# Score products of eight heads summed by identity matmuls one tile ahead, first norm two tiles ahead, w1 parts over ten tiles

## The reference

```python
kv = (ctx @ W_kv.T + b_kv).reshape(B, S, 16, 16, 2); k, v = kv[..., 0], kv[..., 1]
qh = layernorm(x).reshape(B, S, 16, 16)
attn = softmax(einsum('bshd,bstd->bsht', qh, k) / 4, axis=-1)
x = x + tanh(g_xattn) * (einsum('bsht,bstd->bshd', attn, v).reshape(B, S, 256) @ W_out.T + b_out)
y = layernorm(x)
probs = softmax(y @ gate_w.T, axis=-1)            # (16, 256, 8)
g, m = top_k(probs.transpose(0, 2, 1), 64)         # each expert takes 64 tokens of a batch row
h = gelu(y[m] @ w1[e], exact) @ w2[e]              # 256 -> 1024 -> 256
x = x + tanh(g_ffn) * scatter_add(g * h)
```

## Time and profile before

| | us |
|---|---|
| median of 3 runs | 724.87 (723.82 to 727.46) |
| the profiled execution's own time | 725.79 |
| its span, first to last instruction | 723.8 |
| PE busy | 637.5 (88%) |
| VectorE busy | 614.1 (85%) |
| ScalarE busy | 433.7 (60%) |
| POOL busy | 549.6 (76%) |
| mean granted TensorE clock | 0.936 |

### The profile page before, as it was taken

One profiled execution on the slowest core, in us unless ns is written; L12 is line 12 of the kernel. 1 busy time (PEld: TensorE's weight loads), 2 busy tenths in 40 slices (PEclk: granted clock), 3 DMA queues, 4 the chain that ended last, 5 costly groups with the idle time before them and its releaser, 6 DMA issues.

```text
span 723.8 us, 10865 instructions
## 1 busy us (share of the span) xinstructions
PE 637.5 (88%) x3588; PEld 510.6 (71%) x3588; DVE 614.1 (85%) x750; ACT 433.7 (60%) x1079; POOL 549.6 (76%) x497
## 2 busy tenths in 40 slices
PE   5757887644789999998999999989999999999994
PEld 2323433322578888886888888868888899999994
DVE  4999999999999999999899999999999351577762
ACT  5477777644567777785677777847766633232320
POOL 3888888888877888889889888888888615446434
PEclk9887898756799999999999999989999999999998
DMA  6967774413347777777888787768877868999982
GB/s 183 347 225 267 252 262 154 155 62 119 117 161 233 234 237 241 229 220 214 231 250 240 233 235 224 219 219 230 224 222 224 269 171 273 329 307 305 310 234 29
DMA packets 97068, 160.90 MB, mean 222 GB/s; under 512 B 8171, under 2 KB 74486, under 8 KB 97014
## 3 DMA queue, kind: packets, MB, share of 16 engines
q1 hardware_dynamic: 84150, 142.91, 59.4%
q0 software_dynamic: 12288, 16.79, 12.7%
q10 hardware_dynamic: 576, 0.52, 0.2%
HBM read 126.63 MB, written 33.55 MB: 221 GB/s over the span
## 4 chain that ended last, share of the span: by engine, by line
PE 53%; DVE 23%; DMA 9%; issue 6%; POOL 5%; ACT 1%; POOLq 0%; ACTq 0%; DVEq 0%
PE bank L1040 20%; PE bank L1021 19%; DVE prod_v L467 10%; DMA out_dram<-ys,ids 7%; DVE co L469 5%; PE bank L950 5%; DVE S L469 4%; PE bank L970 3%; PE bank L933 2%; PE bank L1009 2%; POOL out_dram L389 2%; POOL prod_p L321 1%; POOL xg L375 1%; PE bank L982 1%; DMA xn_scratch<-xn 1%
## 5 line engine op out<-in xcount | busy, mean ns | idle before, releaser
L1021 PE MATMUL bank<-xin,w1in 128*128 128x256 f32 x1536 | 205.0, 291 | 8.7 <-DVE xin L605 5.6
L1021 PEld LDWEIGHTS bank<-xin,w1in 128*128 128x128 f32 x1536 | 194.0, 197 | 10.3 <-issue 9.7
L1040 PE MATMUL bank<-w2s,hT 128*128 128x256 f32 x768 | 175.4, 382 | 0.0
L389 POOL DMA_INDIRECT out_dram<-ys,ids x64 | 110.1, 1721 | 75.0 <-ACT ys L770 56.6
L1040 PEld LDWEIGHTS bank<-w2s,hT 128*128 128x128 f32 x768 | 142.4, 190 | 17.7
L760 ACT ACTIVATE hT<-bank 128x512 f32<-128x512 f32 x128 | 76.3, 598 | 113.1 <-PE bank L1021 112.7
L469 DVE TENSOR_REDUCE co<-prod_v 128x208 f32<-128x3328 f32 (+2 forms) x32 | 109.7, 3429 | 1.1
L467 DVE TENSOR_TENSOR prod_v<-bank,Ex 128x3328 f32<-128x3328 f32 (+2 forms) x32 | 109.6, 3424 | 0.1
L321 POOL TENSOR_TENSOR prod_p<-kvs,q 128x1024 f32<-128x1024 f32 (+2 forms) x32 | 94.6, 2955 | 12.7 <-ACT q L728 12.6
L467 DVE TENSOR_TENSOR prod_v<-bank,q 128x3072 f32<-128x3072 f32 (+2 forms) x32 | 98.2, 3068 | 6.6 <-ACT q L728 6.6
L469 DVE TENSOR_REDUCE S<-prod_v 128x192 f32<-128x3072 f32 (+2 forms) x32 | 98.2, 3070 | 1.1
(11 more groups left out here) (131 smaller groups left out, 1070.0 us busy)
## 6 DMA issues: line engine op xcount, KB each, us to landing
w1in<-w_parts SPq DMA_DIRECT2D x128, 512.0 KB, 4.8
w2s<-in_L_ffn_w_dram SPq DMA_DIRECT2D x32, 1024.0 KB, 5.8
w_parts<-w1s SPq DMA_DIRECT2D x32, 512.0 KB, 3.5
w1raw<-in_L_ffn_w_dram SPq DMA_DIRECT2D x32, 256.0 KB, 4.4
ct<-in_ctx_dram SPq DMA_DIRECT2D x32, 128.0 KB, 5.3
xt<-in_x_dram SPq DMA_DIRECT2D x32, 128.0 KB, 4.4
out_dram<-x SPq DMA_DIRECT2D x32, 128.0 KB, 4.4
xn_scratch<-xn SPq DMA_DIRECT2D x32, 128.0 KB, 2.7
```

The costliest lines, as they stand in the source:

```text
L389: pool.indirect_dma_start(out=out_rows[:, :], out_offset=bass.IndirectOffsetOnAxis(ap=ids[:, g % 2, p * E + e:p * E + e + 1], axis=0), in_ ...
L1021: ins = pe.matmul(HB[k % 2][:, D * f:D * (f + 1)], w1in[:, k, w, c, P * f:P * (f + 1)].bitcast(f32r), xin[:, n % 2, x_, c, :], start=(m == ...
L1040: ins = pe.matmul(dst, hT[:, n % 2, f, cols], w2s[:, n % 2, f, :], start=(f == 0), stop=(f == FC - 1))
```

## The change

In tiles 1 to 9 the scores of heads 0 to 7 are made one tile ahead and summed on another engine. VectorE writes the products of these eight heads for tile t+1 in two halves of four heads, ordered by channel d first (`summed_products`); the first half stands behind its own score products of tile t and reads the bank of K before ScalarE has copied it, the second stands behind the last subtraction. TensorE adds the 16 slices of 128 columns by 16 identity matmuls into a part of the bank YB (`score_sums`). In tile t+1 VectorE takes maximum and subtraction of these heads from that bank, and of the other eight apart. Its own share is then heads 8 to 11 and POOL's heads 12 to 15 (before: 0 to 10 and 11 to 15). `Sc_count` counts the subtractions, two in a summed tile. The products lie in the space of `hp0`, which the last experts use.

The K and V projection of tile s+1 moves ahead of the transposes of `con` in TensorE's order and now waits for `con` of tile s-1 itself. The first norm is made a tile earlier: statistics of tile s+3, `rsqrt(s + 2)` and, in steps 0 to 9, q of tile s+2; `rs` gets two places and `x_mean` four. The 32 quarters of w1 are spread over steps 0 to 9 as 4, 4, 3, 3, ..., and low parts rotate over three banks instead of four. The order of ScalarE's and TensorE's instructions in steps 0 to 9 is rewritten. From step 10 on only the statistics and `rsqrt` come a tile earlier. The diff, with index changes of `x_mean` and `rs`, semaphores and declarations left out:

```diff
-    EARLY, LATE, ROUTING = (11, 11), (12, 13), (4, 12)
+    START, EARLY, LATE, FIRST_ROUTING, ROUTING = (11, 11), (12, 11), (12, 13), (4, 12), (4, 12)
+    HR = 8
...
+    summed = lambda t: 0 < t < N0 - 1
+    heads = lambda t: (START if t == 0 else FIRST_ROUTING if t == N0 - 1 else EARLY if t < N0 - 1 else
+                       ROUTING if routing(t) else LATE)
+    Sc_count = lambda t: t + 1 + min(t, N0 - 2)
+    quarters = lambda s: [divmod(i, Q) for i in range(3 * s + min(s, 2), 3 * s + 3 + min(s + 1, 2))] if s < N0 - 1 else []
...
+        hp0, prod_s = sb_overlaid(("hp0", [P, FC, BG * CAP], f32r), ("prod_s", [P, DK * HR * DK], fp32))
...
-        LB = HB + [YB, XT]
+        LB = HB + [XT]
+        SP = YB[:, 0:HR * DK]
...
-                if s < E:
-                    for k in range(2):
-                        store_parts(s, k)
-                        if s + 2 < E:
-                            load_raw(s + 2, k)
+                for e, k in quarters(s)[0:1]:
+                    store_parts(e, k)
+                    if e + 2 < E:
+                        load_raw(e + 2, k)
                 if 2 <= s <= NT + 1:
                     store_xn(s - 2)
-                if s < E:
-                    for k in range(2, Q):
-                        store_parts(s, k)
-                        if s + 2 < E:
-                            load_raw(s + 2, k)
+                for e, k in quarters(s)[1:]:
+                    store_parts(e, k)
+                    if e + 2 < E:
+                        load_raw(e + 2, k)
...
-                if n >= 3:
-                    pool.wait_ge(ve_ready, n - 2)
-                if n >= 1:
-                    pool.wait_ge(q_ready, min(n, NT))
                 if n >= 4:
-                    pool.wait_ge(xn_ready, n - 3)
-                pool.tensor_tensor(rs[:, :], ve[:, :], neg_half[:, :], ALU.pow).then_inc(rs_ready, 1)
+                    pool.wait_ge(ve_ready, n - 3)
+                if n >= 2:
+                    pool.wait_ge(q_ready, min(n - 1, NT))
+                if n >= 6:
+                    pool.wait_ge(xn_ready, n - 5)
+                pool.tensor_tensor(rs[:, n % 2, :], ve[:, :], neg_half[:, :], ALU.pow).then_inc(rs_ready, 1)
...
-                    pool.wait_ge(Sc_ready, t)
-                share(H - hk, Kv, qi, S[:, hk * DK:H * DK], 2 * t, Sp_done, t + 1 if routing(t) else None)
+                    pool.wait_ge(Sc_ready, Sc_count(t - 1))
+                share(H - hk, Kv, qi, S[:, hk * DK:H * DK], 2 * t, Sp_done, 1 if t == 0 else t + 2 if routing(t) else None)
...
-                    rsqrt(s + 1)
+                    rsqrt(s + 2)
...
+            def summed_products(t, half):
+
+                h0, h1 = HR // 2 * half, HR // 2 * (half + 1)
+                full = [P, DK, HR // 2, DK]
+                Kp = KV[t % 2][:, 0:D].rearrange("p (t d) -> p d t", d=DK).unsqueeze(2).broadcast_to(full)
+                qi = q[:, t % 2, :].rearrange("p (h d) -> p d h", d=DK)[:, :, h0:h1].unsqueeze(3).broadcast_to(full)
+                pv = prod_s[:, :].rearrange("p (d h t) -> p d h t", d=DK, t=DK)[:, :, h0:h1, :]
+                if half == 0:
+                    dve.wait_ge(kv_psum, t + 1)
+                    dve.wait_ge(q_ready, t + 1)
+                    if t > 1:
+                        dve.wait_ge(sums_psum, t - 1)
+                else:
+                    dve.wait_ge(kvs_ready, t + 1)
+                dve.tensor_tensor(pv, Kp, qi, ALU.mult).then_inc(prods_ready, 1)
...
-                qi = q[:, t % 2, :].rearrange("p (h d) -> p h d", d=DK)[:, 0:hk, :]
+                h0 = HR if summed(t) else 0
+                qi = q[:, t % 2, :].rearrange("p (h d) -> p h d", d=DK)[:, h0:hk, :]
                 Ev = Ex[:, :].rearrange("p (h t) -> p h t", t=DK)
                 dve.wait_ge(kvs_ready, t + 1)
                 dve.wait_ge(q_ready, t + 1)
-                products(hk, Kp, qi, S[:, 0:hk * DK], 2 * t, Sv_done)
+                products(hk - h0, Kp, qi, S[:, h0 * DK:hk * DK], 2 * t, Sv_done)
+                if summed(t + 1):
+                    summed_products(t + 1, 0)
                 if routing(t):
                     choose_tokens(t // TG - 1)
+                if t > 0:
+                    dve.wait_ge(E_ready, t)
+                Sv = S[:, :].rearrange("p (h t) -> p h t", t=DK)
+                Sd = Sc[:, :].rearrange("p (h t) -> p h t", t=DK)
+                if summed(t):
+                    dve.wait_ge(sums_psum, t)
+                    Sm = SP.rearrange("p (h t) -> p h t", t=DK)
+                    dve.reduce_max(sum_max[:, :], Sm, AX.X).then_inc(mx_done, 1)
+                    dve.wait_ge(mx_done, Sc_count(t) - 1)
+                    dve.tensor_tensor(Sd[:, 0:HR], Sm, sum_max[:, :].unsqueeze(2).broadcast_to([P, HR, DK]),
+                                      ALU.subtract).then_inc(Sc_ready, 1)
                 dve.wait_ge(Sp_done, t + 1)
                 dve.wait_ge(Sv_done, t + 1)
-                Sv = S[:, :].rearrange("p (h t) -> p h t", t=DK)
-                dve.reduce_max(row_max, Sv, AX.X).then_inc(mx_done, 1)
-                dve.wait_ge(mx_done, t + 1)
-                if t > 0:
-                    dve.wait_ge(E_ready, t)
-                dve.tensor_tensor(Sc[:, :].rearrange("p (h t) -> p h t", t=DK), Sv,
-                                  row_max.unsqueeze(2).broadcast_to([P, H, DK]), ALU.subtract).then_inc(Sc_ready, 1)
+                dve.reduce_max(row_max[:, h0:H], Sv[:, h0:H], AX.X).then_inc(mx_done, 1)
+                dve.wait_ge(mx_done, Sc_count(t))
+                dve.tensor_tensor(Sd[:, h0:H], Sv[:, h0:H], row_max[:, h0:H].unsqueeze(2).broadcast_to([P, H - h0, DK]),
+                                  ALU.subtract).then_inc(Sc_ready, 1)
+                if summed(t + 1):
+                    summed_products(t + 1, 1)
...
+                if summed(t):
+                    act.wait_ge(prods_ready, 2 * t - 1)
...
-                copy(w1s[:, k, 1], LB[k][:, :].rearrange("p (c f) -> p c f", c=DC), low_made)
+                copy(w1s[:, k, 1], LB[(Q * e + k) % 3][:, :].rearrange("p (c f) -> p c f", c=DC), low_made)
...
+            x_stats(2)
+            make_q(1)
             for s in range(N0 - 1):
+                parts = quarters(s)
                 if s > 0:
                     take_coT(s - 1)
+                make_high(*parts[0])
+                make_high(*parts[1])
                 take_kv(s + 1)
-                if s < E:
-                    make_high(s, 0)
-                    make_high(s, 1)
+                take_low(*parts[0])
                 exponentials(s)
-                if s < E:
-                    take_low(s, 0)
-                    take_low(s, 1)
-                make_q(s + 1)
+                if s + 2 < N0:
+                    make_q(s + 2)
                 if s >= 2:
                     make_xn(s - 2)
-                if s < E:
-                    make_high(s, 2)
-                    make_high(s, 3)
-                x_stats(s + 2)
+                take_low(*parts[1])
+                for part in parts[2:]:
+                    make_high(*part)
                 if s >= 2:
                     take_xnT(s - 2)
-                if s < E:
-                    take_low(s, 2)
-                    take_low(s, 3)
+                if s >= 1:
+                    x2_stats(s - 1)
+                x_stats(s + 3)
                 if s >= 2:
                     take_logits(s - 2)
+                take_ctT(s + 2)
                 if routing(s + 1):
                     gate_exp(s // TG - 1)
-                take_ctT(s + 2)
-                if s >= 1:
-                    x2_stats(s - 1)
+                for part in parts[2:]:
+                    take_low(*part)
...
-                if t >= 2:
+                if 2 <= t < N0:
+                    pe.wait_ge(con_ready, t - 1)
+                elif t >= 2:
...
-                if e > 0:
-                    pe.wait_ge(low_made, Q * (e - 1) + k + 1)
-                pe.matmul(LB[k][:, :], ident[:, :], w1raw[:, e % 2, k].rearrange("p c f -> p (c f)"), start=True, stop=False)
-                pe.matmul(LB[k][:, :], minus_ident[:, :], w1s[:, k, 0].rearrange("p c f -> p (c f)"),
+                i = Q * e + k
+                if i >= 3:
+                    pe.wait_ge(low_made, i - 2)
+                pe.matmul(LB[i % 3][:, :], ident[:, :], w1raw[:, e % 2, k].rearrange("p c f -> p (c f)"), start=True, stop=False)
+                pe.matmul(LB[i % 3][:, :], minus_ident[:, :], w1s[:, k, 0].rearrange("p c f -> p (c f)"),
                           start=False, stop=True).then_inc(low_psum, 1)
+
+            def score_sums(t):
+
+                pe.wait_ge(prods_ready, 2 * t)
+                if t > 1:
+                    pe.wait_ge(Sc_ready, Sc_count(t - 1))
+                for d in range(DK):
+                    ins = pe.matmul(SP, ident[:, :], prod_s[:, HR * DK * d:HR * DK * (d + 1)], start=(d == 0), stop=(d == DK - 1))
+                ins.then_inc(sums_psum, 1)
...
```

(43 more changed lines are left out.)

12 lines of the change are left out of this document (6 added, 6 removed).

## The result

The changed kernel takes 718.94 us (median of 5 runs, 716.97 to 719.42), the kernel before 726.59 beside it (5 runs): a ratio of 0.9903 with a 95% interval of 0.9888 to 0.9919, 7.65 us less at the median. The forecast was 8.6 us less. The profiled execution spans 717.0 us against 723.8, at a mean granted clock of 0.969 against 0.936. The ratios in this document leave out slow runs, of which there was one: of the six runs of the kernel with the low part's copy behind q and xn, one took 1099.27 us at a mean granted clock of 0.555 (their median of 714.35 us includes it).

A forecast was written before the change was run, and what follows sets the result against it. VectorE was taken to bound tiles 0 to 9, TensorE from tile 11 on. Tile 0 +1.6, tiles 1 to 8 -8 x 1.05, tile 9 -1.8 sum to -8.6 us: 716.3 us, range 711.5 to 727.5.

The forecast's parts named there:

- VectorE's passes: VectorE in tiles 1 to 8: scores 4.68, maximum and subtraction 1.08, residual and denominator 0.74, values 6.74; 13.24 us without waits.
- The waits: VectorE in tiles 1 to 8: first half under 0.1, second 0.1, residual 0.3; 0.45 us more, period 13.7.
- the weight load of 0.19: Rival, TensorE's sums: loads of 0.19 us each make them 6.1 us, TensorE's loop 15.6; +6.6, 731.5 us; chance 0.04.
- Strided reads, the slower rival: Summed products reading K one element in 16: a half costs 0.88 us more, period 15.3; +6.0, 731 us; chance 0.12.
- Low clock: Rival: TensorE's clock still falls for 3 us of a tile, making its 13.4 us 14.9; +1, 726 us; chance 0.14.
- Tile 0 and set-up: Tile 0 pays two summed halves, 2.28 us, less 0.6 or more of exponential and hops: +1.6 us.
- Tile 9, the mis-sized term: Tile 9 makes no sums for a next tile; VectorE's work falls to 11.0 us, saving 1.8 us against 14.76.
- POOL's loop of 12.97 decides: Tile 9: POOL's values, scores, subtraction wait, exponential and restart, 12.97 us, set the tile's time.
- The layout's own chain of TensorE: Steady tile, from the written context: projection to 2.3, transposes 2.6, first low part 3.6 to 4.9, output projection to 6.1 us.
- First norm two tiles ahead: Changes no steady tile: as many statistics, `rsqrt` and q as before, and ScalarE's chain has room.
- nothing on the queues: SP's queue: parts stored up to a tile later cost nothing; if the lead were used up, 4 to 5 us once.
- The sum: Whole kernel: +1.6 - 8 x 1.05 - 1.8 = -8.6 us, giving 716.3 us for the median; chance 0.58.

The follow-up runs named there:

- the best version: Against the changed kernel: output projection ahead of the first low part, that part's copy behind q and xn, reciprocal in free columns of YB; 711.34 us, ratio 0.9799.
- where the exponential came later: Changed kernel with TensorE's output projection moved ahead of the step's first low part, ScalarE's order kept; 720.63 us, ratio 0.9935.
- the same kernel: Changed kernel with 1 of the 16 identity matmuls of each tile's sums, the other fifteen channels left out; 741.51 us, ratio 1.0218.

## Why the prediction was right, and where not

- **VectorE's passes.** Right throughout. The passes of 1024 were put at 1.22 us and took it; the sum of all, 13.24, is 13.16 where no wait is left (the best version), and 13.80 less the waits of 0.61 in the changed kernel.
- **The waits.** First half 0.15 (under 0.1 forecast), second 0.11 (0.1), residual 0.35 (0.3). The period of 13.80 lies 0.1 above the 13.7, which over eight tiles is the 0.8 us by which the steady tiles save less (7.63 against 8.4). The residual was laid out at 6.2 us behind `con` and came at 6.25.
- **POOL.** S was forecast at 4.0 of the tile and wanted then; it ended at 90.05, 4.07 behind `con`, wanted at 90.10. That there is no slack was shown where the exponential came later.
- **TensorE.** The sums took 3.74 us in place of 3.9, by the price of the transposes; the weight load of 0.19 did not pace them.
- **Strided reads, the slower rival.** Excluded: 1.22 and 1.23 us against 1.22 for the same count in order. The Trainium skill's page "Advanced Engine Details and Errata" (section "Memory Cachelines") wants every two consecutive elements in PSUM contiguous for best throughput, and names matmuls alone as slowed. The forecast's reading of it, a penalty for VectorE too, does not agree with this trace, and the measurement decides.
- **Low clock.** It did not come about: TensorE waits at most 0.99 us at a time in the steady tiles, and the clock is 1.00 in every stretch from 42 to 140 us. But that rested on the length of the sums in a way the forecast did not see, and the fall would have cost far more than the +1 us it was priced at: the two kernels that leave out the sums, or most of them, show 0.67 in some stretches and take 744 and 741 us.
- **Tile 0 and set-up.** +1.40 in place of +1.6, and +0.34 of set-up put at nothing.
- **Tile 9, the mis-sized term.** Forecast -1.8, measured -0.95. The step that failed is "POOL's loop of 12.97 decides": the tile took 14.19 from `con` to `con`. The layout's own chain of TensorE, 6.1 us to the output projection, holds in tile 9 too and sets the residual at 6.33 us behind the start. With the exponential alone moved forward, which makes POOL earlier and leaves that chain, tile 9 stays at 14.19. Where that chain is shorter (the low part behind the output projection, or none in the tile) tile 9 takes 12.79 and 12.76 from `con` to `con`, against 14.19 in the changed kernel and 15.14 before: a saving of 2.4, even over the 1.8. That 15.14 shows a bit of luck: the forecast took tile 9 of the kernel before at the 14.76 of a steady tile, but two passes of the routing stand in it. So the tile came out 1.22 us above the 12.97, and 0.38 of it did not show in the saving. VectorE's timeline of the kernel before:

```profile
146.66 0.42 DVE L518 TENSOR_TENSOR con<-co,bank 128x256 f32<-128x256 f32 x1
...
161.80 0.42 DVE L518 TENSOR_TENSOR con<-co,bank 128x256 f32<-128x256 f32 x1
```

- **First norm two tiles ahead; the order of the parts.** Nothing in a steady tile for the one, as the waits show no engine held by it; it was not undone alone. For the parts "nothing on the queues" held, and the 1.2 us a tile taken off TensorE in tiles 2 to 7 turned out worth nothing in the total.
- **The sum.** -8.6 forecast; the first expert matmul came at 178.66 us (near 177 forecast); the spans show -6.8 and the medians -7.65. Of the 1.8 between forecast and spans, 0.85 is tile 9, 0.8 the waits of the steady tiles, and 0.34 set-up, less 0.2 in tile 0. The median lies 2.6 us above the 716.3 forecast, but 1.7 of that is the kernel before, which came at 726.59 beside it and not at 724.87.

## What to carry to other kernels

Where work is handed from the bound engine to another, lay out the helper's whole chain in each kind of tile, the last one too: a freed engine waits for whatever was just in time. Filling an engine with short work can pay twice if it shortens the idle stretch behind which its clock falls, so trying the new order without the new work can look worse than the old kernel. Before a scratch operand moves from PSUM to SBUF to save a wait, see what the other engine on SBUF is running then.

## What the runs showed of the hardware that was not expected

- A VectorE product with both inputs in SBUF took 1.37 and 6.22 us beside POOL's running products of 2.36 and 6.65 us, ending 0.28 and 0.27 us behind them; with one input in PSUM it took 0.42 us beside such a product.
- TensorE's idle of 3.1 us was followed by a granted clock of 0.50, and the four instructions of the KV projection took 3.75 us in place of 1.95, while a wait of 2.80 us in the same kernel was followed by 1.00 and 1.95 us; in the changed kernel, where TensorE waits at most 0.99 us from 42 to 130 us, the clock stayed at 1.00. So 3.5 us less work a tile for TensorE made the kernel 23 us slower.
- VectorE's product reading its bank at a step of 16 elements took 1.22 us for 1024, as in order.
